# Turning routed and scored rows in 32x32 blocks on VectorE in place of TensorE, with outputs in two alternating banks

## What is computed

```python
# layer 0: mix the 64 channels of a sample, then a dense layer with 8 experts of rank 16
y  = einsum('bct,bcd->bdt', x, L0_cond_weights[cond])        # 64x64 per sample
p  = top-2 of softmax(y @ W_gate.T), renormalised            # 8 experts, 2 used
hw = (y @ A.T) * p            # 128 = 8 experts x 16 ranks: the "routed rows"
x1 = x + y @ W_base.T + b_base + hw @ B
# layer 1: an adapter per sample, then 8 experts of rank 16, all used
z  = x1 @ L1_cond_weight[adapter].T
s  = 8 * softmax(z @ Wr.T + br)
lw = (z @ A1.T) * s           # the "scored rows"
out = x1 + 2 * lw @ B1
```

## Time and profile before

| | |
|---|---|
| time, median of 3 runs | 736.33 us (735.84 to 737.25) |
| profiled execution, its time | 735.89 us |
| span from its first to its last instruction | 734.2 us |
| TensorE (PE) busy | 719.7 us, 98% |
| VectorE (DVE) busy | 340.5 us, 46% |
| ScalarE (ACT) busy | 113.8 us, 16% |
| GpSimd (POOL) busy | 57.8 us, 8% |
| mean granted TensorE clock | 0.998 of full |

### The profile page before, as it was taken

The page is one execution under the profiler, slowest core; times in us unless marked ns, Lnnn a source line. Parts: engine busy times, 40 slices in busy tenths (PEclk is TensorE's granted clock), DMA queues, the critical chain, the costliest instruction groups (busy, mean ns, idle before and its releaser), DMA issues.

```text
span 734.2 us, 12343 instructions
## 1 busy us (share of the span) xinstructions
PE 719.7 (98%) x4502; PEld 645.3 (88%) x4502; DVE 340.5 (46%) x887; ACT 113.8 (16%) x309; POOL 57.8 (8%) x115
## 2 busy tenths in 40 slices
PE   8999998999999999999999999999999999999996
PEld 8999997898889988898889888988889888998996
DVE  2000296056525554465426561655346543674644
ACT  2222300031102110022003200311012100320111
POOL 1222310001100010001000110001000000010100
PEclk9999999999999999999999999999999999999999
DMA  7899991506654467248714764447634782395542
GB/s 281 319 417 385 385 411 31 223 4 193 235 207 166 143 229 283 101 135 295 280 74 177 233 242 186 174 138 238 261 122 146 244 298 87 144 340 205 221 185 72
DMA packets 38705, 156.23 MB, mean 213 GB/s; under 512 B 8837, under 2 KB 11909, under 8 KB 28421
## 3 DMA queue, kind: packets, MB, share of 16 engines
q1 hardware_dynamic: 27714, 78.72, 28.2%
q0 software_dynamic: 9216, 71.31, 28.2%
q10 hardware_dynamic: 1730, 5.58, 1.9%
HBM read 133.24 MB, written 22.35 MB: 212 GB/s over the span
## 4 chain that ended last, share of the span: by engine, by line
PE 90%; DVE 4%; DMA 2%; SPq 2%; issue 1%; ACT 0%; POOLq 0%; DVEq 0%
PE base_ps L339 17%; PE base_ps L340 17%; PE base_ps L341 17%; PE base_ps L348 8%; PE out_ps L408 4%; PE low_ps L408 4%; PE mix_both L362 4%; PE mix_both L373 3%; PE out_ps L362 2%; PE low_ps L362 2%; PE out_ps L339 2%; PE out_ps L340 2%; PE out_ps L341 2%; DVE w_lo L681 1%; PE low_ps L373 1%; PE out_ps L373 1%
## 5 line engine op out<-in xcount | busy, mean ns | idle before, releaser
L339 PE MATMUL base_ps<-yT,w_hi 128*128 128x512 f32 (+1 forms) x576 | 213.6, 371 | 1.3 <-DVE xT L801 1.1
L341 PE MATMUL base_ps<-yT,w_hi 128*128 128x512 f32 (+1 forms) x576 | 211.6, 367 | 0.0
L340 PE MATMUL base_ps<-yT,w_lo 128*128 128x512 f32 (+1 forms) x576 | 211.4, 367 | 0.0
L339 PEld LDWEIGHTS base_ps<-yT,w_hi 128*128 128x128 f32 x576 | 108.4, 188 | 21.2 <-DVE xT L801 4.0
L341 PEld LDWEIGHTS base_ps<-yT,w_hi 128*128 128x128 f32 x576 | 108.4, 188 | 18.1
L340 PEld LDWEIGHTS base_ps<-yT,w_lo 128*128 128x128 f32 x576 | 108.5, 188 | 15.8
L840 DVE TENSOR_TENSOR xT<-xT,out_ps 128x512 f32<-128x512 f32 (+1 forms) x53 | 35.4, 668 | 102.8 <-PE out_ps L341 102.8
L348 PE MATMUL base_ps<-ag_raw,stage 128*128 128x136 f32 x640 | 75.2, 280 | 1.6 <-DMA stage<-in_w 1.0
L348 PEld LDWEIGHTS base_ps<-ag_raw,stage 128*128 128x128 f32 x640 | 74.4, 190 | 2.5 <-issue 1.4
L950 POOL DMA_DIRECT2D adapter<-folded x60 | 31.9, 532 | 564.7 <-PE low_ps L408 491.3
L697 DVE TENSOR_TENSOR x1T<-xT,x1T 128x256 fp32r<-128x256 f32 x120 | 45.4, 420 | 59.5 <-ACT x1T L571 59.5
(11 more groups left out here) (158 smaller groups left out, 848.0 us busy)
## 6 DMA issues: line engine op xcount, KB each, us to landing
adapter<-folded POOLq DMA_DIRECT2D x63, 1088.0 KB, 5.4
stage<-in_w SPq DMA_DIRECT2D x40, 512.0 KB, 7.6
x_rows<-in_x SPq DMA_DIRECT2D x32, 512.0 KB, 8.8
xT<-in_x_turned SPq DMA_DIRECT2D x16, 1024.0 KB, 6.0
out<-xT SPq DMA_DIRECT2D x28, 512.0 KB, 2.7
folded<-adapter ACTq DMA_DIRECT2D x10, 544.0 KB, 6.7
w_raw<-in_w SPq DMA_DIRECT2D x8, 256.0 KB, 8.1
w_raw<-in_w SPq DMA_DIRECT2D x4, 512.0 KB, 12.0
```

Of the source, the lines that this page charges most:

```text
L339: pe.matmul(dst, st_hi, mv_lo, start=start, stop=False, skip_group_check=True)
L340: pe.matmul(dst, st_lo, mv_hi, start=False, stop=False, skip_group_check=True)
L341: return pe.matmul(dst, st_hi, mv_hi, start=False, stop=stop, skip_group_check=True)
```

## The change

Both turns leave TensorE. VectorE does each in 16 instructions, each of which turns four 32x32 blocks (one per tile) from `rows` into the place in SBUF where the unturned numbers were (`hg` for the routed, `lg` for the scored rows); ScalarE and VectorE then read SBUF and not PSUM. `turn_hw` stands on VectorE behind `sum_low(2)` of the first half, `turn_lw` right behind the scoring. With `low_ps` free of turned rows the outputs alternate between `low_ps` and `out_ps`: two behind k = 3, one behind 4, two behind 5, one behind 6, two behind 7, all ahead of `delta(1)`. An output now waits for the `final` two ahead of it. The last 256 tokens' turns (`turn_lw(0, last, …)` with half the tiles, and `turn_tail`) stay on TensorE.

```diff
+        hw_turned = hg[:, :, 0:HR]
+        lw_turned = lg[:, :, 0:HR]
...
+        def by_tile(columns):
+            return columns.rearrange("p (t n) -> p t n", n=P)
...
-            def turn_hw(q, r):
-                pe.wait_ge(route_step, at(q, r, ROUTE_STEPS, ROUTE_STEPS))
-                for t in range(TILES):
-                    mm = pe.transpose(mix_ps[0][:, t * P:(t + 1) * P], rows[:, t, :], identity[:, :])
-                mm.then_inc(hwT_done, 1)
...
-                    if k == 5:
-                        turn_hw(q, r)
...
-                    if l1 and k == 1:
-                        turn_lw(q, r - 1)
-                    if l1 and k >= 2:
-                        make_out(q, r - 1, k - 2, out_ps[:, :], k - 2)
-                if l1:
-                    make_out(q, r - 1, KC - 2, low_ps[:, :], 0)
+                    if l1:
+                        for n in ((), (), (), (0, 1), (2,), (3, 4), (5,), (6, 7))[k]:
+                            make_out(q, r - 1, n, low_banks[n % 2][:, :], max(n - 1, 0))
                 delta(1, toks)
-                if l1:
-                    make_out(q, r - 1, KC - 1, out_ps[:, :], KC - 2)
...
-                act.copy(hwT[:, 0, :], mix_ps[0][:, :]).then_inc(hwT_hi_done, 1)
+                act.copy(by_tile(hwT[:, 0, :]), hw_turned).then_inc(hwT_hi_done, 1)
...
+            def turn_rows(turned, done):
+
+                for tok in range(0, P, BLOCK):
+                    for rank in range(0, P, BLOCK):
+                        block_turned = dve.transpose(turned[rank:rank + BLOCK, :, tok:tok + BLOCK],
+                                                     rows[tok:tok + BLOCK, :, rank:rank + BLOCK])
+                block_turned.then_inc(done, 1)
+
+            def turn_hw(q, r):
+                dve.wait_ge(route_step, at(q, r, ROUTE_STEPS, ROUTE_STEPS))
+                turn_rows(hw_turned, hwT_done)
+
+            def turn_lw(q, r):
+                dve.wait_ge(score_step, at(q, r, SCORE_STEPS, SCORE_STEPS))
+                turn_rows(lw_turned, lwT_done)
...
                     for i in range(2, PER):
                         x1T_low(q, r - 1, i)
                         sum_low(q, r - 1, i - 2)
+                        if i == 4:
+                            turn_hw(q, r)
+                else:
+                    turn_hw(q, r)
                 hwT_low(q, r)
...
                     scoring(q, r - 1)
+                    turn_lw(q, r - 1)
                 if l1:
                     lwT_low(q, r - 1)
-                    for n in range(KC - 2):
-                        final(q, r - 1, n, out_ps[:, :])
-                    final(q, r - 1, KC - 2, low_ps[:, :])
+                    for n in range(KC):
+                        final(q, r - 1, n, low_banks[n % 2][:, :])
                 for n in range(HALF, KC):
                     add_base(q, r, n, toks)
-                if l1:
-                    final(q, r - 1, KC - 1, out_ps[:, :])
```

More of the change, by code:

```diff
@@ L209, in build @@
         SCORE_STEPS = 8
+        BLOCK = 32
         SIDES = KC + 1 + 4 + 1
@@ L583, in lwT_high @@
                 act.wait_ge(lwT_done, at(q, r, 1, 1))
-                act.copy(lwT[:, 0, toks], low_ps[:, toks]).then_inc(lwT_hi_done, 1)
+                if toks == ALL:
+                    act.copy(by_tile(lwT[:, 0, :]), lw_turned).then_inc(lwT_hi_done, 1)
+                else:
+                    act.copy(lwT[:, 0, toks], low_ps[:, toks]).then_inc(lwT_hi_done, 1)
             def iteration(q, r, l1=True):
@@ L784, in scoring @@
                                   ALU.mult).then_inc(score_step, 1)
+            def turn_rows(turned, done):
[10 more added lines that the diff above has]
+                turn_rows(lw_turned, lwT_done)
             def hwT_low(q, r):
                 dve.wait_ge(hwT_hi_done, at(q, r, 1, 1))
-                dve.tensor_tensor(hwT[:, 1, :], mix_ps[0][:, :], hwT[:, 0, :], ALU.subtract).then_inc(hwT_lo_done, 1)
+                dve.tensor_tensor(by_tile(hwT[:, 1, :]), hw_turned, by_tile(hwT[:, 0, :]), ALU.subtract).then_inc(hwT_lo_done, 1)
             def lwT_low(q, r, toks=ALL):
                 dve.wait_ge(lwT_hi_done, at(q, r, 1, 1))
-                dve.tensor_tensor(lwT[:, 1, toks], low_ps[:, toks], lwT[:, 0, toks], ALU.subtract
-                                  ).then_inc(lwT_lo_done, 1)
+                if toks == ALL:
+                    dve.tensor_tensor(by_tile(lwT[:, 1, :]), lw_turned, by_tile(lwT[:, 0, :]), ALU.subtract
+                                      ).then_inc(lwT_lo_done, 1)
+                else:
+                    dve.tensor_tensor(lwT[:, 1, toks], low_ps[:, toks], lwT[:, 0, toks], ALU.subtract
+                                      ).then_inc(lwT_lo_done, 1)
             def add_base(q, r, n, toks=ALL):
```

## The result

The changed kernel takes 751.61 us (749.75 to 753.3, 6 runs) where the kernel before, run beside it, takes 736.84 us (735.84 to 738.26): a ratio of 1.0202, 95% interval 1.0186 to 1.0217. It is slower by 2.0%, and the forecast of 736.5 us, its range of 730.3 to 741.0 included, was wrong. The profiled execution took 751.03 us with a span of 749.3 us; before it was 735.89 and 734.2.

A forecast was written before the change was run, and what follows sets the result against it. TensorE, busy 98% of the span, was taken as the bound. Six middle passes -5.3 us, first pass +0.7, last +2.0 and +2.8 sum to +0.2: 736.1 profiled, 736.5 us median, with a range of 730.3 to 741.

The forecast's parts named there:

- The price of a turn on TensorE: A turn of four transposes costs TensorE 0.44 us; 12 turns removed from the six middle passes save 5.3 us.
- T: Time of 16 block turns on VectorE: 5.3 us at 0.33 each; forecast case 4.7 to 5.55, chance 0.42.
- held for the reason given: On VectorE, each block turn writes another partition quarter, so it waits until the one before is done: 0.33 us each.
- due times of both chains: Middle passes: block turns stay hidden up to 5.5 us for routed rows at `make_low(5)`, 6.2 for scored rows at output 0.
- the wait for the adapter's DMA: Last pass, `make_low(7)`: the old wait for this load, landed at 659.33, goes as TensorE arrives later; net +2.0 us there.
- The three waits: TensorE waits about 3.5 us at first-pass `delta(0)`, and in the last pass 3.6 at `make_low(5)`, 3.4 at output 0.
- (a): Block turns overlap on VectorE, wholly or except where the read quarter changes: T 3.3 to 3.8, 730.5 to 732; chance 0.32.
- (b): Block turns slower, so `make_low(5)` waits in each middle pass: 741 at T 5.9, 761 at 7.4; chance 0.26.
- the sum's middle passes: Six middle passes counted alike, both chains hidden behind TensorE's work, saving 12 turns of 0.44 us: -5.3 us.
- is no new wait: Output 7 ahead of `delta(1)` puts its `final` ahead of `add_base(4)` on VectorE; it ends about when that is due: no cost.
- a wait in `mix`: Listed as what would make the forecast wrong: waits at outputs or there, which it held for hidden; no size given.
- the ends: First and last pass: the first changes by +0.7 us, the last by +2.0 and +2.8, giving back the middle passes' gain.

The follow-up runs named there:

- 32 halves: Changed kernel with VectorE's loop written out and each block turn cut into two of 64 elements; 747.12 us, ratio 1.0141 to the kernel before.
- late loads: Changed kernel with SyncE holding the next pass's x loads until 7 of that pass's 8 mix chunks are done; 744.06 us, ratio 1.0102.
- without any turn: Kernel before, turns on TensorE, with the change's output banks and order and 64 one-column memsets in VectorE's loop body; 741.9 us, ratio 1.008.
- written-out kernel: Changed kernel with VectorE's loop over passes 1 to 6 written out, no jump back; 738.7 us, ratio 1.006 to the kernel before.
- the kernel with 12 memsets: Kernel before with the change's output banks and order, turns on TensorE, and 12 one-column memsets in VectorE's loop body; one execution, 736.16 us.
- padded kernel: Kernel before with 64 one-column memsets more in VectorE's loop body, 16 at each place of the block turns; 736.72 us, ratio 1.0019.

## Why the prediction was wrong

**Right.** The price of a turn on TensorE, 0.44 us, was right: a middle pass without a disturbance is 0.9 to 1.0 us shorter, with 0.88 forecast. So was the block turn: 0.315 us for 0.33, and T 5.05 for 5.3, held for the reason given (6.01 us for 32 halves, and their starts). The Trainium skill, VectorE: DVE Perf Modes, § Two Vector instructions with no wait between them, says that a change of the output's start quadrant alone holds an instruction; the trace agrees, with 0.205 to 0.21 us from start to start where the written quarter changes and 0.16 to 0.175 where it doesn't. The 311 ns that the Trainium skill gives in VectorE: DVE Perf Modes, § The three transpose paths, are for 128x128 in bf16, in 32x32 blocks. A turn of 32 partitions x 128 f32 measures 303 ns here. The due times of both chains in the middle passes held, the wait for the adapter's DMA in the last pass is gone, and the banks are neutral. The three waits are each 0.3 to 0.4 us under the forecast: 0.25 because T was shorter, the rest because the profile counts from the modelled end of the matmul before. Rivals (a) and (b) both fell: T is neither under 4.7 nor over 5.5.

**The step that failed first: the sum's middle passes.** It took them as six times the same, and asked of each moved piece only which engine waits for it. I wrote of output 7 that its `final` "is no new wait". That is so on VectorE; but the same `final` releases the last store and with it SyncE's loads of x, which are the next thing on the DMA engines. That I left unfollowed, although elsewhere I had followed what is queued behind a piece. The prediction does name a wait in `mix` as a sign that it would be wrong, but gives it no price. And of the 64 added instructions I counted only their running time, not that they stand in a loop's body. Together they cost 2 x 4.4 us, which is shown by taking away either half (passes 3 and 5 at 78.4 and 78.6 us with late loads, 77.9 without the loop) and by making the stall without any turn (6.4 us). The Trainium skill, Runtime: NRT & Kernel Launch, § Instruction fetch mechanics, says that a taken branch to a target outside the engine's two-page window of instructions forces a DMA fetch before work can go on. The trace agrees in kind: there is a fetch packet at each jump, and 22 packets in all on the instruction queue, with a body of 347 or 349 instructions, and none at a jump, with 12 or 13 in all, with 283 to 315. The Trainium skill gives that window as 512 instructions in pages of 256; no run here shows what decides between 315 and 347. Behind the 2 MB of loads the stall was 4.4 to 5.2 us over all runs.

**The step that failed next: the ends.** The waits had their forecast sizes, and were priced at these. Behind them TensorE ran at half clock for 3.4 us at a time: 1.7 us in the first pass and 4.0 in the last that the sum had at nothing. Filling the waits with idle work gave back 1.6 and 1.5 us (the written-out kernel had one stretch in each pass), and taking the waits away in the last pass 8.8. The kernel before had a wait of 2.1 us at full clock, and I read no more from it than that; in another execution, of the kernel with 12 memsets, half clock followed the same wait and cost 1.6 us. So a single profile did not show the price.

**Open.** Half clock followed some waits of 2.1 to 3.4 us and not others: after two alike ones of 2.40 us in one execution it came once. In the middle of passes 2, 4 and 6 of the changed kernel, behind `delta(0)`, the first `add_base` of VectorE starts 0.3 us late, which it does not with the loop written out; nothing in the trace names its cause. Where the limit lies between 315 and 347, and whether it depends on where the body starts, was not tried. Why VectorE goes on only 1.9 us behind the fetch packet is not known either.

## What to carry to other kernels

Count instructions added to an engine's loop as well as their time: here, between 315 and 347 in the body, each jump back began to need a fetch by DMA, and where 2 MB of loads had been put ahead of it the engine stood for 4.4 us and more instead of 2.3. When an instruction moves earlier, follow what it releases to the last queue: here an add that ended sooner moved 2 MB of loads in front of a fetch. A wait that opens on TensorE costs its length and sometimes half as much again in clock behind it; so move work off TensorE only where the other engine's chain is hidden, and leave it there where it is not, pass by pass.

## What the runs showed of the hardware that I had not expected

- An instruction fetch shares the DMA engines with data and got no precedence here: alone, at 310.2 us of the padded kernel, it made VectorE idle for 2.3 us; among x loads (365 GB/s) its packet came 2.5 to 3.3 us behind the jump and not 0.3 to 0.6, and the idle time was 4.4 to 5.2.
- Transposes of an identity, 24 in 2.78 us, were enough to keep the granted clock at 1.00 through what would have been a wait of 3.1 us.
- A block turn of 32 partitions x 128 f32 takes VectorE 303 ns, 0.315 us from start to start, as the written quarter changes each time. Sixteen of them are 5.05 us for what four transposes in TensorE's stream do in 0.44.
